# Decayed attention with its projections moved into the time scan, in a six-layer fp32 perceiver on Trainium2

## What is computed

```python
q, k, v = x @ Wq.T, x @ Wk.T, x @ Wv.T
b = (q * k).sum(-1) / 8                  # one number per token and head
a = -softplus(x @ Wa.T + ba).sum(-1)     # log of the decay, per token and head
# scan over the 64 steps, kept in logs with a sign in the reference:
#   lse   <- log(exp(a_t + lse) + exp(b_t))
#   state <- exp(a_t) * state + exp(b_t) * v_t     (with an eps of 1e-8 in the logs)
#   y_t   = sum over heads of state / exp(lse)
out = y @ Wo.T
```

## Time and profile before

| | |
|---|---|
| runs shown | 2339.34 to 2342.31 us, median 2342.2 |
| the profiled execution | 2338.0 us, of it the span of the core 2336.1 |
| TensorE busy | 2090.7 us (89%), mean granted clock 0.91 of full speed |
| VectorE, ScalarE, GpSimd busy | 1084.3, 930.7, 121.7 us |
| layer 4 | 808 to 1694 us |
| layer 5 | 1694 to 2068 us: projections to 1815, exchange through DRAM to 1844, scan to 2034, output product to 2068 |
| layer 6 | 2068 to 2336 us |

### The profile page before, as it was taken

One profiled execution on the slowest core, in us unless ns is written; L12 is line 12 of the kernel. 1 busy time (PEld: TensorE's weight loads), 2 busy tenths in 40 slices (PEclk: granted clock), 3 DMA queues, 4 the chain that ended last, 5 costly groups with the idle time before them and its releaser, 6 DMA issues. The chain is left out here.

```text
span 2336.1 us, 30096 instructions
## 1 busy us (share of the span) xinstructions
PE 2090.7 (89%) x9904; PEld 1465.4 (63%) x9904; DVE 1084.3 (46%) x2172; ACT 930.7 (40%) x1699; POOL 121.7 (5%) x138
## 2 busy tenths in 40 slices
PE   7978962999999779999999999999979499877999
PEld 4647762555555467787877778787757377633444
DVE  4655552010100145345252625344355599739992
ACT  5743320111111144445444545544344477615550
POOL 0000013000000011000000000000000000002220
PEclk9989965999999989999999999999989555588999
DMA  7410024778878421100000101010021700000000
GB/s 259 127 44 1 0 116 170 302 289 311 317 282 317 169 85 61 40 27 27 27 27 27 40 14 40 13 49 19 1 91 45 254 1 1 1 5 0 1 14 23
DMA packets 35591, 212.41 MB, mean 91 GB/s; under 512 B 5059, under 2 KB 5060, under 8 KB 27974
## 3 DMA queue, kind: packets, MB, share of 16 engines
q1 hardware_dynamic: 32966, 203.28, 23.1%
q0 software_dynamic: 2560, 8.39, 1.1%
HBM read 189.04 MB, written 22.61 MB: 91 GB/s over the span
## 5 line engine op out<-in xcount | busy, mean ns | idle before, releaser
L106 PE MATMUL PS<-cT,qs 128*128 128x512 f32 x1152 | 293.7, 400 | 7.0 <-ACT pb L1212 7.0
L106 PE MATMUL PS<-pT,cN 128*128 128x512 f32 x1152 | 271.8, 394 | 1.7 <-DVE pT L1309 1.7
L898 PE MATMUL PS<-W,xgT 128*128 128x384 f32 x736 | 243.2, 489 | 1.4 <-ACT xgT L921 1.4
L106 PEld LDWEIGHTS PS<-cT,qs 128*128 128x128 f32 x1152 | 208.4, 188 | 57.3 <-issue 15.1
L106 PEld LDWEIGHTS PS<-pT,cN 128*128 128x128 f32 x1152 | 215.0, 189 | 46.0 <-DVE pT L1309 1.9
L898 PEld LDWEIGHTS PS<-W,xgT 128*128 128x128 f32 x736 | 140.6, 191 | 104.5 <-issue 11.8
L1207 ACT ACTIVATE qp<-PS 128x512 f32<-128x512 f32 x192 | 110.9, 596 | 198.4 <-PE PS L106 191.4
L106 PE MATMUL PS<-ws,xT 128*128 128x512 f32 x672 | 170.2, 412 | 11.0 <-DVE ws L1533 6.0
L1304 DVE TENSOR_REDUCE nmax<-PS 128x1 f32<-128x512 f32 x128 | 87.7, 685 | 158.5 <-PE PS L106 158.1
L106 PEld LDWEIGHTS PS<-ws,xT 128*128 128x128 f32 x672 | 131.8, 199 | 46.3 <-issue 17.8
L949 DVE TENSOR_TENSOR hid<-gated,PS 128x384 f32<-128x384 f32 x46 | 23.4, 551 | 278.0 <-PE PS L874 235.6
(11 more groups left out here) (227 smaller groups left out, 3154.5 us busy)
## 6 DMA issues: line engine op xcount, KB each, us to landing
W<-in_fc SPq DMA_DIRECT2D x23, 3072.0 KB, 12.7
W<-in_proj SPq DMA_DIRECT2D x23, 1536.0 KB, 6.8
cT<-in_ctxT SPq DMA_DIRECT2D x16, 768.0 KB, 5.6
ct_in<-in_ctxT SPq DMA_DIRECT2D x16, 768.0 KB
cn_in<-in_ctxN SPq DMA_DIRECT2D x16, 768.0 KB
W<-in_w SPq DMA_DIRECT2D x2, 4096.0 KB, 24.6
routed_x<-zero SPq DMA_DIRECT2D x23, 256.0 KB, 5.4
xg<-routed_x SPq DMA_DIRECT2D x23, 256.0 KB, 5.9
```

The source lines that it names most:

```text
L106: mm = nc.tensor.matmul(out, lhs(m, s), rhs(n, s), start=(opens and (s, m, n) == terms[0]), stop=((s, m, n) == terms[-1]))
L898: mm = nc.tensor.matmul(ps[c][:, 0:HFE], xgT[:, k, :], fc[u][:, k, c * HFE:(c + 1) * HFE], start=(k == 0), stop=(k == DK - 1))
```

## The change

**Layer 4.** `queries_through_Wk` has 6 steps instead of 12. A step works on two banks, one per half of the rows, and its matmuls alternate between the halves; ScalarE empties one bank and VectorE the other. TensorE enters it after `oT` has been taken. The value product swaps its two inner loops. SyncE also stores every finished tile of x in DRAM (`x_d`), and loads the V, alpha and Q weights of layer 5 during the last tile.

```diff
 def queries_through_Wk(i):                       # TensorE
+    pe.wait_ge(e_sb, BASE + PAIRS * i + 2)
+    for step in range(QP):                       # QP = 6
+        n, c = divmod(step, CK)
+        if step >= 2:
+            pe.wait_ge(qp_act, BASE + QP * i + step - 1)
+            pe.wait_ge(qp_dve, BASE + QP * i + step - 1)
+        for m in range(4):
+            for r in range(2):
+                part = slice(r * DH1, (r + 1) * DH1)
+                mm = nc.tensor.matmul(qp_banks[step % 2][r][:, m * P:(m + 1) * P],
+                                      wk4[part, 4 * n + m, c * P:(c + 1) * P],
+                                      qT[part, 4 * n + m, :], start=True, stop=True)
+        mm.then_inc(qp_mm, 1)
...
+    taken(use + U_O + 1, 3)                      # tile(), before, not after:
     if not last:
-        queries_through_Wk(i + 1, use + U_QP, U_QP, 3)
-
-    taken(use + U_O + 1)
+        queries_through_Wk(i + 1)
...
+def queries_through_Wk(i):                       # VectorE, ScalarE alike for r = 0
+    for step in range(QP):
+        ve.wait_ge(qp_mm, BASE + QP * i + step + 1)
+        heads, src = through(step, 1)
+        nc.vector.tensor_copy(heads, src).then_inc(qp_dve, 1)
```

```diff
+ORDER = (W5_V, W5_A, W5_Q, W5_K)
...
+    for c in range(NG):                          # TensorE
+        for j in range(G):
+            t = G * c + j
+            if t + AHEAD < S:
+                values(t + AHEAD)
+            if j == 0 and c + 1 < NG:
+                project(c + 1, W5_A)
+            elif j == 1 and c + 1 < NG:
+                project(c + 1, W5_Q)
+            elif j == 2 and c + 1 < NG:
+                project(c + 1, W5_K)
+            elif j == 3 and c + 2 < NG:
+                turn_x(c + 2)
+            elif j == 4 and c + 1 < NG:
+                by_head(c + 1)
+            elif j == 5 and c >= 1:
+                out_proj(c - 1)
+            elif j == 7 and c + 2 < NG:
+                project(c + 2, W5_V)
+            head_sums(t)
+    out_proj(NG - 1)
...
+                        if j == 0:               # ScalarE, behind bv, ebv and ear of the step
+                            if c >= 1:
+                                take_y(c - 1)    # waits for head_sums(8 c - 1)
+                            if c + 1 < NG:
+                                take_v(c + 1)
+                        elif j == 1 and c + 1 < NG:
+                            take_a(c + 1)        # Abs, Exp, Ln; waits for project(c + 1, W5_A)
+                        elif j == 2 and c + 1 < NG:
+                            take_q(c + 1)
+                        elif j == 4 and c + 2 < NG:
+                            turned_x(c + 2)
+                        elif j == 6 and c + 1 < NG:
+                            exponents(c + 1)
...
+                        if j == 0 and c + 2 < NG:      # VectorE, between s and the maximum
+                            stats(c + 2)
+                        elif j == 3 and c + 1 < NG:
+                            products(c + 1)
+                        elif j == 5 and c + 2 < NG:
+                            turned_x(c + 2)
+                        elif j == 6 and c >= 1:
+                            add_out(c - 1)
+                        elif j == 7 and c + 1 < NG:
+                            weights(c + 1)
...
+                        if j == 1 and c + 2 < NG:      # VectorE, between the maximum and the sign
+                            ln.vector_norm(ve, c + 2)
+                        if j == 1 and c + 1 < NG:
+                            make_v(c + 1)
+                        elif j == 2 and c + 1 < NG:
+                            softplus(c + 1)
+                        elif j == 5 and c + 1 < NG:
+                            by_head(c + 1)
+                            logs(c + 1)
```

```diff
                 sp.dma_start(w_in[:, 3], a["w5"][:, W5_K]).then_inc(s_wk, 16)
                 sp.dma_start(bal[:, :], a["ba5"]).then_inc(s_bal, 16)
+                sp.wait_ge(e.s_xd, BASE + 16 * NT)
...
                 sp.dma_start(b1[:, :], a["b16"]).then_inc(s_b, 16)
+                sp.dma_start(w26, a["w26"]).then_inc(s_w26, 16)
                 sp.dma_start(b2[:, :], a["b26"]).then_inc(s_b, 16)
```

More of the change, by code:

```diff
@@ L1236, in weighed, with queries, queries_through_Wk @@
                              count=final if c == CK - 1 else 1)
-                def queries(use, which):
+                def queries(use, which, final=1):
                     for n in range(2):
[L1240 to L1254, removed]
+                        take(use + n, which + n, qT[:, 4 * n:4 * n + 4, :].rearrange("p m t -> p (m t)"), SCALE,
+                             final if n else 1)
+                def queries_through_Wk(i):
+                    for step in range(QP):
+                        act.wait_ge(qp_mm, BASE + QP * i + step + 1)
+                        heads, src = through(step, 0)
+                        nc.scalar.activation(heads, src, ACT.Copy).then_inc(qp_act, 1)
+                    act.wait_ge(qp_act, BASE + QP * (i + 1))
+                    act.wait_ge(qp_dve, BASE + QP * (i + 1))
+                    for g in range(QB):
+                        first_q(i, g)
                 def tile(i, last):
@@ L1591, in decayed_attention_layer @@
-        HALVES = slice(0, D // 2), slice(D // 2, D)
+        w_in = W0[:, 0:4 * DK * D].rearrange("p (w k n) -> p w k n", w=4, k=DK)
+        ws = [sbuf(f"ws5{part}", [P, 4, DK, D], F32R) for part in range(2)]
+        vt = W0[:, 8192:8192 + NG * D].rearrange("p (c d) -> p c d", c=NG)
+        wo = W0[:, 12288:12288 + DK * D].rearrange("p (k n) -> p k n", k=DK)
+        rb = W0[:, 14336:14336 + RB * D].rearrange("p (n d) -> p n d", n=RB)
+        pick = sbuf("pick5", [P, CN_ALL - CN_PICK])
+        same, eight = pick[:, G * P:(G + 1) * P], pick[:, (G + 1) * P:(G + 1) * P + G]
@@ new lines, in _ @@
+                rest_w(2)
+                rest_w(3)
+                stats(1)
+                ln.vector_norm(ve, 1)
+                make_v(0)
+                softplus(0)
+                ve.wait_ge(s_pick, BASE + 16)
+                products(0)
+                turned_x(1)
+                by_head(0)
+                logs(0)
+                weights(0)
+                ve.wait_ge(coef, BASE + 1)
+                ve.sem_inc(r_sb, 2)
+                for c in range(NG):
+                    for j in range(G):
+                        t = G * c + j
+                        old, new = rb[:, (t - 1) % RB, :], rb[:, t % RB, :]
+                        ve.wait_ge(bv_sb, BASE + t + 1)
+                        for h, cols in enumerate(HALVES):
+                            ve.wait_ge(r_sb, BASE + 2 * t + h + 1)
+                            nc.vector.scalar_tensor_tensor(s_[:, cols], old[:, cols], al[:, t:t + 1], bv[:, t % 2, cols],
+                                                           ALU.mult, ALU.add).then_inc(s_sb, 1)
+                        if j == 0 and c + 2 < NG:
[8 more added lines that the diff above has]
+                            weights(c + 1)
+                        ve.wait_ge(ebv_sb, BASE + VB + t + 1)
```

640 lines of the change are left out of this document (316 added, 324 removed).

## The result

The changed kernel takes 2301.2 us (median of 4 runs, 2300.7 to 2303.6) against 2341.4 us before: a ratio of 0.983, 95% interval 0.9815 to 0.9849. Forecast: 2306. The profiled run has a span of 2298.8 us, 37.3 less than before.

A forecast was written before the change was run, and what follows sets the result against it. TensorE was taken to bound layer 4 and layer 5's first and last pieces, VectorE the scan. Layer 4 -21, layer 5 -24 and layer 6 +11 gave -34 on 2338.0: 2304, predicted median 2306, range 2265 to 2362.

The forecast's parts named there:

- Layer 4, -21: Layer 4: 21 us saved, mainly from Wk product records at 60 ns in place of 86; bounds nothing and 27.
- First s 40 us behind layer 4: Layer 5 up to the scan's first s: 40 us, between 30 and 55, in place of 151.9; 112 saved.
- Scan 300: Layer 5's scan: 300 us, 112 more than now, from floor 253, ScalarE waits 24 and clock lateness 23.
- The floor of 253: Scan on VectorE: 179.8 us of steps plus 73 us of added work over seven chunks.
- The 24 us for ScalarE at j = 0 and 1: Scan: VectorE waits behind ScalarE's table load, alpha wait and take_y, 3.5 us a chunk, 24 us.
- the rival built on 2.66 us a switch: Scan: each of 14 table switches hides a 1.38 us drain, 19 us more, time 2325; chance 0.06.
- 23 us for clock lateness: Scan: a third of TensorE's work at half clock delays take_y and take_a, adding 23 us.
- the clock stays up: scan 272: Scan rival: thin stretches short enough, only floor and ScalarE waits count; 28 us less, time 2278; chance 0.20.
- A: Reading after the result: VectorE's 42 us of scan waits are single latencies, each curable where it stands.
- B: Reading after the result: TensorE's in-order work and clock set each chunk's pace; curing one of the 42 us of waits makes another.
- Layer 6, +11: Layer 6 start: b2 queued behind w26 costs 10.8 us, half-size output transfers 0.4; 11 us lost, between 0 and 15.
- Slower rival: Scan: half-clock V and alpha products hold ScalarE and VectorE 6 to 8 us a chunk; 2356 at scan 350; chance 0.14.

The follow-up runs named there:

- experiment 5: Changed kernel with the product through Wk in its old order, four matmuls of one row half and then four of the other: 2315.8 us.
- experiment 3: Changed kernel with ScalarE's copy of y moved from j = 0 to j = 3: 2302.0 us.
- experiment 4: Changed kernel with Exp in place of Ln on ScalarE, so no table load in the scan (decays differ): 2302.0 us.
- experiment 12: Changed kernel with output product at j = 3, b2 ahead of w26, and 3, 7 and 4 idle matmuls at j = 4, 5, 6: 2263.6 us.
- experiment 2: Changed kernel with VectorE's addition of the output product moved from j = 6 to j = 2 of the next chunk: 2285.8 us.
- experiment 7: Changed kernel with the V product at j = 6 in place of 7 and alpha at j = 7 in place of 0: 2314.3 us.
- experiment 6: Changed kernel with three idle matmuls added behind the head sums at j = 3, 4 and 6: 2303.0 us.
- experiment 9: Changed kernel with the output product moved on TensorE from j = 5 to j = 3, into the bank of V and Q: 2295.2 us.

## Why the prediction was right, point by point

- *Layer 4, -21: was -14.5.* Mechanism right (experiment 5), sizes off: a record takes 64 ns, not the 60 taken, so the records gave 16.8 us, not 20. The bank wait went as said, but the waits as a whole rose from 6.3 to 7.7 us and did not fall by half a microsecond. VectorE's copies, put at nothing, come with 2.0 us of waits for L1337; the swapped loops gave 2.1 back. The bound of 27 us was no reading of the factor of two. The Trainium skill (TensorEngine Tiling (Array Packing), Theoretical Speedup) has "Up to 2×" for a small dimension of at most 64. The prediction halved the 86 ns, in which the two halves already overlapped in part. Against the 119 ns of a record with all 128 rows, 64 ns is a factor of 1.86, close to the page's two; against the 83 ns of experiment 5 it is 1.3.
- *First s 40 us behind layer 4: was 36.9.* 3 less; its four terms were not measured one by one.
- *Scan 300: was 290.4*, with some luck in the parts. The floor of 253 was 6 too high: the 290.4 less 40.5 of waits and 3 of small ones is 247. The 24 us for ScalarE at j = 0 and 1 were 18.5 of waits for bv within the scan, where expected but not for the reason given: experiments 3 and 4 took away take_y's place and the table load and gained nothing. TensorE's in-order products end those waits. The table load followed by Ln 0.02 us after its end has no drain in its row here either, and all 14 switches are worth nothing; the rival built on 2.66 us a switch falls.
- *23 us for clock lateness: were 22*, which is luck: the 23 is worked out from no row, and the wait is one that the text did not name. It placed the lateness at take_y and take_a; it was at j = 6, an output product issued at half clock one step ahead of its reader. Working: a third of TensorE's work was taken at half clock, which by the prediction's own sum would be a mean clock of some 0.75 over the scan (an estimate: 147 us at full and 143 at half clock); the granted mean was 0.88. The list of rivals had "the clock stays up: scan 272". Experiment 12 comes near that case, with the output product at j = 3: 264.8. Of the two readings, A holds for most of the wait at j = 6 (moving the addition in experiment 2 gave 15.4 us) and B for the waits at j = 1 to 3 (experiments 3 and 4).
- *Tail 10: was 10.1. Layer 6, +11: was +13.5.* The wait for b2 rose by 10.6 us (4.2 to 14.8), as priced (10.8); issuing b2 first took 10.3 of it away. It was not "in place of nothing". From the end of VectorE's last operation to the end of the span are 3.7 us in place of 2.4: with the last output in two transfers, 1.3 us, where 0.4 was taken. No run separates the other 1.6.
- *Sum -34 on the profiled execution: was -37.3.* The errors were +6.5 in layer 4, -3, -10 and +2.5: they cancel in part, and the total is nearer than its parts.
- *Slower rival, from 336 us of scan on:* nothing came near; the worst order (experiment 7) reached 296.6.

What stays open: no run has the filling matmuls on the unchanged order, or the later additions of experiment 2 with b2 first (2274 if their gains add, an estimate from the two). Experiments 6 and 12 differ in number, steps and place of the added matmuls and in the order of the products, so what it takes to hold the clock is not shown. Of experiment 12's remaining wait for bv at j = 2 (1.8 us a chunk) no run shows how much would be left to the K product.

## What to carry to other kernels

When work is moved beside a chain of small dependent steps, add up each engine's in-order program over one whole period, with its clock, before costing single waits: a wait that is cured comes back elsewhere if another engine is full (experiment 4; in experiment 2 a quarter of it did). Where TensorE has thin steps between dense ones, look at the granted clock in windows of a few microseconds; if half clock comes once a period, reordering the products moves it to another of them (6 us less to 13 more here), and filling the pauses, the largest above all, can be worth more than any order (24 us). Of a bulk transfer and a small one on the same queue, issue first the small one if the next stage waits for it (11.3 us here).

## What the runs showed that was not expected

- A pause of 1.73 us, behind thin steps at full clock, was followed by some 10 us at half clock, although TensorE was busy in all of them (1896.90 to about 1907, experiment 9). With 14 matmuls of 0.33 us a chunk in the pauses the clock stayed at 0.99 and the kernel was 24 us faster for doing more.
- Alternating the 64-row half at each matmul brought an fp32 record of 128 columns from 83 to 64 ns, against 119 ns with all 128 rows.
- The addition of the output product in the last chunk waited 5.8 us, four times its shortest wait in the others: without the projections TensorE stayed at half clock there, and was slower in a bare step (3.4 us) than VectorE (2.8).
